# Key features of a linear-attention layer: squaring, casts and norm products in another order, and one graph tile routed later

## The reference, cut to what matters

```python
xn = layernorm(x)                                   # x: 3125 nodes x 768
# (a) two graph convolutions: D^-1/2 (A + I) D^-1/2 (h W^T) + b, ReLU between them
# (b) linear attention over all nodes, 12 heads of 64, 256 random features:
q, k, v = split(xn @ W_qkv)
phi(t) = exp(t @ rf.T - 0.5 * sum(t * t)) / 16
kv   = sum_n phi(k)[n] x v[n];  ksum = sum_n phi(k)[n]
attn = (phi(q) @ kv) / (phi(q) @ ksum + 1e-6) @ W_proj + b_proj
x = x + gcn2(relu(gcn1(xn))) + layernorm(xn + attn)
# (c) a mixture of experts: each row goes to one of 8 experts
logits = layernorm(x) @ router_w.T;  e = the larger index of the top two
x = x + silu(layernorm(x) @ w1[e]) @ w2[e]
```

## Time and profile before

| | us |
|---|---|
| median of 3 executions | 2439.72 (2438.98 to 2440.8) |
| profiled execution, its own time | 2437.48 |
| span of its trace | 2435.7 |
| PE busy | 2339.3 (96%) |
| DVE, ACT, POOL busy | 1262.1, 870.8, 868.5 |
| busy time of line 387 / 1884 on PE | 897.1 / 813.9 |
| mean granted TensorE clock | 0.989 of full speed |

### The profile page before, as it was taken

The page is one execution under the profiler, slowest core; times in us unless marked ns, Lnnn a source line. Parts: engine busy times, 40 slices in busy tenths (PEclk is TensorE's granted clock), DMA queues, the critical chain, the costliest instruction groups (busy, mean ns, idle before and its releaser), DMA issues.

```text
span 2435.7 us, 44796 instructions
## 1 busy us (share of the span) xinstructions
PE 2339.3 (96%) x16783; PEld 1584.5 (65%) x16783; DVE 1262.1 (52%) x2843; ACT 870.8 (36%) x1323; POOL 868.5 (36%) x615
## 2 busy tenths in 40 slices
PE   5999999999999999999999999999999999999697
PEld 3878787878666666665666666666665566666375
DVE  6757575735667676766214344344431444444444
ACT  3546464634737374553113222222220111111143
POOL 1001215567778777776630112111100000000166
PEclk9999999999999999999999999999999999999899
DMA  7778786654331313224336767767755465554287
GB/s 280 284 279 290 259 275 163 171 129 81 66 66 1 65 0 65 26 27 98 59 55 224 238 204 219 225 205 214 227 172 197 141 213 177 201 181 156 74 184 141
DMA packets 172421, 385.63 MB, mean 158 GB/s; under 512 B 74800, under 2 KB 81818, under 8 KB 166396
## 3 DMA queue, kind: packets, MB, share of 16 engines
q1 hardware_dynamic: 90220, 313.83, 37.2%
q0 software_dynamic: 71264, 40.45, 15.0%
q10 hardware_dynamic: 10800, 29.50, 3.1%
HBM read 222.76 MB, written 166.44 MB: 160 GB/s over the span
## 4 chain that ended last, share of the span: by engine, by line
PE 78%; DVE 7%; ACT 7%; issue 4%; POOL 1%; DMA 1%; SPq 1%; DVEq 0%; ACTq 0%; POOLq 0%
PE pair L1884 33%; PE pair L387 31%; PE pair L1702 5%; PE pair L1682 2%; DVE arena L1337 2%; DVE arena L1339 2%; DVE arena L1343 2%; ACT arena L941 2%; PE pair L1632 2%; PE pair L1691 1%; ACT arena L872 1%; POOL out_rows L795 1%; PE pair L1804 1%; ACT arena L951 1%; ACT arena L878 1%
## 5 line engine op out<-in xcount | busy, mean ns | idle before, releaser
L387 PE MATMUL pair<-arena 128*128 128x384 f16 (+2 forms) x5760 | 897.1, 317 | 5.3 <-issue 3.4
L741 POOL DMA_INDIRECT cells<-arena x392 | 660.5, 1685 | 563.9 <-DMA cells<-arena 430.0
L1884 PE MATMUL pair<-arena 128*128 128x384 f16 x4900 | 813.9, 326 | 0.9 <-DVE arena L1503 0.9
L387 PEld LDWEIGHTS pair<-arena 128*128 128x128 f16 x5760 | 563.7, 98 | 321.2 <-issue 7.7
L1884 PEld LDWEIGHTS pair<-arena 128*128 128x128 f16 x4900 | 474.0, 98 | 306.7 <-issue 2.1
L773 POOL DMA_INDIRECT slots<-arena x25 | 28.8, 1150 | 484.4 <-DVEq L1558 451.8
L1702 PE MATMUL pair<-arena 128*128 128x66 f32 x1200 | 157.8, 275 | 4.9 <-ACT arena L912 4.5
L1702 PEld LDWEIGHTS pair<-arena 128*128 128x128 f32 x1200 | 146.7, 192 | 13.7 <-ACT arena L912 11.4
L912 ACT ACTIVATE arena<-pair,arena 128x256 f32<-128x256 f32 x300 | 123.8, 473 | 67.4 <-PE pair L1682 64.9
L1012 ACT ACTIVATE arena<-arena 128x768 f32<-128x768 f32 x25 | 23.4, 935 | 334.5 <-DVE arena L1437 334.5
L759 POOL DMA_DIRECT2D arena<-cells x25 | 30.3, 1213 | 293.3 <-DMA arena<-cells 286.7
(11 more groups left out here) (202 smaller groups left out, 2451.5 us busy)
## 6 DMA issues: line engine op xcount, KB each, us to landing
cells<-arena SPq DMA_DIRECT2D x50, 800.0 KB, 9.6
ahl_dram<-arena SPq DMA_DIRECT2D x23, 1600.0 KB, 10.7
arena<-ahl_dram SPq DMA_DIRECT2D x23, 1600.0 KB, 7.7
arena<-in_x SPq DMA_DIRECT2D x70, 384.0 KB, 3.9
arena<-key_dram SPq DMA_DIRECT2D x28, 896.0 KB, 5.8
arena<-cells SPq DMA_DIRECT2D x25, 800.0 KB, 7.4
arena<-cells POOLq DMA_DIRECT2D x25, 800.0 KB, 7.7
split_w<-arena SPq DMA_DIRECT2D x32, 384.0 KB
```

Of the source, the lines that this page charges most:

```text
L387: ins = nc.tensor.matmul(dst[half], left(k, a), right(k, b, half), start=start and n == 0, stop=stop and n == 2)
L741: nc.gpsimd.indirect_dma_start(cells[k], bass.IndirectOffsetOnAxis(ap=idx_all[:, m:m + 1], axis=0), val_all[:, m:m + 1], None, bounds_chec ...
L1884: ins = nc.tensor.matmul(pair[u][:, half, 0:HD], a[:, 0, s * P:(s + 1) * P], X[part][:, s, half * HD:(half + 1) * HD], start=(s == 0 and p ...
```

## The change

In the key pairs: ACT's cast_k becomes square_k (stands where cast_k stood, after exponential 1) and two single casts, one after exponential 2 and one after exponential 3. The square now raises k_norm, each cast raises k_cast, and DVE's low_k waits for each cast on its own. The eviction of line 833 moves from behind exponential 3 to behind exponential 4. PE issues k_sums(p, 4) first and k_norms(p + 1) behind it, and k_norms also waits for the square. The numbers that k_norm is compared with are adapted. In the prologue of a chunk (pair 0) the square stands ahead of its two casts, with nothing between. In graph layer 2 the tile n = 2, and only it, takes the routing of tile 0 at s = 11, 15 and 22 in place of 1, 5 and 12.

```diff
+            def square_k(c, p):
                 s, j = slot_use[("k", p)]
                 act.wait_ge(slot_full[s], c * uses[s] + j + 1)
-                for h in range(2):
-                    rows = slice(h * DH, (h + 1) * DH)
-                    nc.scalar.copy(halves_of(kh[p % 2][rows, h, :]), bank_pair(s)[rows])
-                nc.scalar.activation(halves_of(ksq[p % 2]), bank_pair(s), ACT.Square).then_inc(k_cast, 1)
+                nc.scalar.activation(halves_of(ksq[p % 2]), bank_pair(s), ACT.Square).then_inc(k_norm, 1)
+
+            def cast_k(c, p, h):
+                s, j = slot_use[("k", p)]
+                rows = slice(h * DH, (h + 1) * DH)
+                nc.scalar.copy(halves_of(kh[p % 2][rows, h, :]), bank_pair(s)[rows]).then_inc(k_cast, 1)
...
                         if t == 1 and p + 1 < PAIRS:
-                            cast_k(c, p + 1)
-                        if more and t == 3 and p:
+                            square_k(c, p + 1)
+                        if t in (2, 3) and p + 1 < PAIRS:
+                            cast_k(c, p + 1, t - 2)
+                        if more and t == TC - 1 and p:
                             evict_lo((c + 1) * TC + p - 1)
...
             def low_k(c, p):
-                dve.wait_ge(k_cast, c * PAIRS + p + 1)
                 for h in range(2):
+                    dve.wait_ge(k_cast, 2 * (c * PAIRS + p) + h + 1)
...
             def k_norms(c, p):
                 pe.wait_ge(k_low, 2 * (c * PAIRS + p) + 2)
+                pe.wait_ge(k_norm, 3 * (c * PAIRS + p) + 1)
...
                     for t in range(TC):
+                        k_sums(c, p, t)
                         if t == TC - 1 and p + 1 < PAIRS:
                             k_norms(c, p + 1)
-                        k_sums(c, p, t)
...
-                    if s == 1:
+                    late = isinstance(n, int) and n == 2
+                    if s == (11 if late else 1):
                         route_turn(n - 2, u)
-                    if s == 5:
+                    if s == (15 if late else 5):
                         route_logits(n - 2)
-                    if s == 12:
+                    if s == (22 if late else 12):
                         route_prefix(n - 2)
```

More of the change, by code:

```diff
@@ L852, in _ @@
             halves_of = lambda ap: ap.rearrange("p (a b) -> p a b", a=2)
-            def cast_k(c, p):
+            def square_k(c, p):
                 s, j = slot_use[("k", p)]
                 act.wait_ge(slot_full[s], c * uses[s] + j + 1)
-                for h in range(2):
-                    rows = slice(h * DH, (h + 1) * DH)
-                    nc.scalar.copy(halves_of(kh[p % 2][rows, h, :]), bank_pair(s)[rows])
-                nc.scalar.activation(halves_of(ksq[p % 2]), bank_pair(s), ACT.Square).then_inc(k_cast, 1)
+                nc.scalar.activation(halves_of(ksq[p % 2]), bank_pair(s), ACT.Square).then_inc(k_norm, 1)
[3 more added lines that the diff above has]
+                nc.scalar.copy(halves_of(kh[p % 2][rows, h, :]), bank_pair(s)[rows]).then_inc(k_cast, 1)
             def norms_k(c, p):
                 s, j = slot_use[("k", p)]
-                act.wait_ge(k_norm, 2 * (c * PAIRS + p) + 1)
+                act.wait_ge(k_norm, 3 * (c * PAIRS + p) + 2)
                 nc.scalar.copy(knorm[:, p % 2, :], pair[s][:, 0, HW:HW + 2 * TC]).then_inc(k_norm, 1)
-                act.wait_ge(k_norm, 2 * (c * PAIRS + p) + 2)
+                act.wait_ge(k_norm, 3 * (c * PAIRS + p) + 3)
                 act.sem_inc(slot_free[s], 2)
@@ L901, in _ @@
                             act.wait_ge(key_stored, 16)
-                        cast_k(c, 0)
+                        square_k(c, 0)
+                        cast_k(c, 0, 0)
+                        cast_k(c, 0, 1)
                         if more:
@@ L1756, in chunk1 @@
                         pe.wait_ge(q_in, 16 * K)
-                        pe.wait_ge(k_norm, 2 * UNITS)
+                        pe.wait_ge(k_norm, 3 * UNITS)
                         q_up(0, 0)
```

## The result

| | before | after |
|---|---|---|
| median (lowest to highest) | 2439.4 (2438.43 to 2442.24) | 2449.86 (2449.05 to 2452.59) |
| executions of this comparison | 6 | 6 |
| span of the profiled execution | 2435.7 | 2448.0 |
| mean granted TensorE clock | 0.989 | 0.984 |

After over before is 1.0046, with a 95% interval of 1.0034 to 1.0058: 10.5 us slower. The forecast was 3.5 us slower. The time lies at the upper edge of the range, and the sign is right; the size is wrong by a factor of three.

A forecast was written before the change was run, and what follows sets the result against it. PE, busy 96% of the span, was taken as the bound, so only its waits or clock count; +4.5 (key pairs) - 6.1 (graph layer 2) + 5.1 (clock) = +3.5 us on the median 2439.72 gave 2443.2, range 2435 to 2450.

The forecast's parts named there:

- The wait moves from sums 2 to sums 4: Key pairs: sums 4 wait instead of sums 2; +0.32 us in 16 pairs, -0.07 in 9, together +4.5 us.
- The degrees 1.19 us behind the norm products: Key pairs on PE: the degrees follow the norm products after 1.19 us, a step not in the trace.
- The swap hides a wait of half a microsecond for low_k: Key pairs: without PE's new order low_k would be late by half a microsecond for the norm products.
- Graph layer 2, -6.1 us: Start of graph layer 2: the turning's 4.97 us wait and the lower clock behind it go, -6.1 us.
- Rival 4: Graph layer 2 keeps half its stall, as tile 3's turning has only 0.5 us to spare: 2446, chance 0.06.
- The clock, +5.1 us: Phase 1: longer narrow runs on PE bring 3 more falls of the clock, 1.7 us each, +5.1 us.
- I take twice as many as now, 3 more: Phase 1: the assumed number of added clock falls, where the earlier trace had three behind 25 runs.
- The bound that the prediction named and didn't take: Phase 1: a clock fall behind half the pairs, 9 more, +15 us.
- each run stands at the edge of a fall: Phase 1: all 25 narrow runs look alike and three were followed by a clock fall, so each is near one.
- Rival 3: Key pairs: longer narrow runs drop the clock behind every second or third pair, 7 falls more: 2450.0, chance 0.17.
- Rival 1: Phase 1: no more clock falls, since PE waits more but the narrow work is the same: 2438.1, chance 0.25.
- Rival 2: Key pairs: the waits at the sums vanish, 10.0 us saved, with 6.1 from layer 2: 2423.6, chance 0.07.

The follow-up runs named there:

- the key part alone: The changed kernel with the routing of tile 2 in graph layer 2 put back, so only the key pairs are changed: 2460.29 us, ratio 1.0084.
- e4: The kernel before with only PE's order swapped, norm products behind sums 4: 2456.59 us, ratio 1.0068.
- e9: The kernel before with only the square moved, from behind the casts to behind exponential 2: 2436.34 us, ratio 0.9971.
- e8: The kernel before with the square behind exponential 4, norm products behind the next pair's first features, and the later layer 2 routing: 2446.3 us, ratio 1.0033.

## Why the prediction was right in its terms and wrong in its size

- **The wait moves from sums 2 to sums 4: right.** 15.0 us in 30 waits, a little over the 11 to 14 that were said to show it; +0.32 and -0.07 a pair, as worked out from the earlier trace rows. The chain on ACT was 2.79 us, forecast 2.83. The second cast overlaps nothing: from exponential 3 to exponential 4 it is 1.57 us (243.29 to 244.86) against 1.30 with the first (241.99 to 243.29).
- **The degrees 1.19 us behind the norm products: right** (246.64 to 247.85 is 1.21).
- **The swap hides a wait of half a microsecond for low_k: right**, shown by the run without it (0.54).
- **Graph layer 2, -6.1 us: right** (-5.94 in after, and no fall at 1895 any more). Tile 3's turning had 0.26 us to spare, not 0.5: low(1) ended at 1924.63 and the turning stood at 1924.89. Rival 4 was near but didn't come.
- **The clock, +5.1 us: the step that failed.** The kind of cost was right: the narrow run became longer, 4.13 us, and the clock fell more often behind it. Its size was not. "I take twice as many as now, 3 more" had no row behind it. There were 6 more behind the pairs, +9.2 us, where +5.1 stood. Beyond these the sum had nothing for falls elsewhere: two more in phase 3 and one at the end go with the remaining +5.1 us between the spans (0.82, 3.00 and 1.27 in the table), and not all of that is shown to come from the change, since falls near 1107 to 1178 come and go from kernel to kernel. So the spans add up to +4.5 - 5.9 + 9.2 - 0.7 + 5.1 = +12.2 of the 12.3 measured. The bound that the prediction named and didn't take, 9 more for +15, is what the key part alone shows (12 against 3). The count of now, 3 of 25, was no measure for what comes. That "each run stands at the edge of a fall" fits the jump from 3 or 4 falls to 12 for a quarter of a microsecond (e4), but nothing in the rows told it beforehand.
- **Rival 3, 7 falls more, 2450.0: this is what happened**, at 2449.86, by six falls more behind the runs and three elsewhere; that the time agrees to 0.1 us is luck, since its 7 falls were to lie behind the pairs and the count differs from trace to trace. Rival 1 (no more falls) fell with the first trace. Rival 2 (both waits vanish) was excluded for the order of the change, rightly, but another order of the same instructions nearly does it (e9, pairs of 13.88 and 13.27, 7.3 of the 10.0 us).
- **What the Trainium skill says.** The run with the norm products doubled has no idle row, PE busy 4.00 of 4.00 us, and 1.2 GHz behind it. The Trainium skill, TensorE: Matmul & The Clock Gate, section HAM oscillation — how this bites in real kernels, puts falls of the clock down to idle gaps of PE between tiles. The measurement goes beyond that here, as the earlier trace rows did: no gap was needed. And the kernel with a gap of 0.38 us in a short run had none behind its pairs 0 to 4.

What stays open: how many falls a given kernel has is not fixed by the length of its run alone (3, 4 and 1 at 3.6 us; 9 and 12 at 4.1), which of the 25 equal runs they follow was not explained, how much the wait inside the run adds wasn't parted, and why falls appear in other phases when phase 1 ends earlier wasn't tried.

## What to carry to other kernels

Where PE is the bound, read the granted clock behind every run of narrow matmuls, and count the places where it falls against the places where it could: a few falls among many equal runs may mean that many stand near the edge (here 3 of 25 became 9 to 12). Before you lengthen such a run, price the falls at up to half of the runs, and see whether some narrow work that nobody waits for can go among wide matmuls instead; here 14 matmuls moved took 16 us back from the changed kernel, though only 1.9 from the kernel before, where few falls stood. Of a chain of small operations on a busy engine, move the one whose reader comes last (the square, 7.8 us faster), not those that others read first (the casts).

## What the runs showed of the hardware that I had not expected

A busy TensorE drops to 1.2 GHz behind narrow work: after 3.6 to 4.7 us of products with 66, 2 and 50 columns the granted clock read 0.57 to 0.59 over the next four microseconds at busy 4.00 of 4.00, and such a fall made its pair about 1.66 us longer (15.73 against 14.07, 16.06 against 14.39). Most often the clock was back within those four microseconds. In two pairs 5 of e8, where sums and features in turn followed a wait of 1.1 us, it stayed at 0.50 for more than eight, and the pair took 15.34 instead of 10.34 us. No run shows what makes the difference.

On ACT the cast of rows 0 to 63 lets the next row start after 0.57 of its 0.68 us (242.72 to 243.29), the cast of rows 64 to 127 after 0.71 of its 0.69 (244.15 to 244.86): one overlaps the next instruction, the other doesn't, and all 25 casts of each kind in after do the same within 0.01 us. Why was not tried.
